# Loading w1 on ScalarE's DMA queue behind x's second half, and x's fourth half directly behind the third

## The reference

```python
q_emb = relu(q @ W3 + b3)
c = relu(((n * v + sum_over_sequence(v)) * q_emb[:, None, :]) @ W2 + b2)      # v = x, n = 32
def ternary_quant(w):
    s = mean(abs(w))
    return clip(round(w / s), -1, 1) * s
h1 = c @ ternary_quant(w1).T                                                  # w1, w3: 682 x 256
h3 = c @ ternary_quant(w3).T
x = x + (silu(h1) * h3) @ ternary_quant(w2).T                                 # w2: 256 x 682
```

## Time and profile before

| | |
|---|---|
| time, median of 3 runs | 165.83 us (165.24 to 166.05) |
| the profiled execution | 165.95 us, its span 164.2 us |
| TensorE (PE) busy | 159.7 us, 97% of the span |
| VectorE (DVE) busy | 116.4 us, 71% |
| ScalarE (ACT) busy | 89.6 us, 55% |
| GpSimd (POOL) busy | 55.1 us, 34% |
| granted TensorE clock | 1.000 of full speed |
| moved by DMA | 12.67 MB, 8.32 MB read and 4.19 MB written |

### The profile page before, as it was taken

How to read it: one execution, slowest core, us unless ns; L and a number is a source line. 1 busy time by engine, 2 the same in 40 slices (tenths; PEclk the granted TensorE clock), 3 DMA queues, 4 the chain that set the end, 5 groups by cost and what they waited for, 6 DMA issues and landing times.

```text
span 164.2 us, 2295 instructions
## 1 busy us (share of the span) xinstructions
PE 159.7 (97%) x764; PEld 131.1 (80%) x764; DVE 116.4 (71%) x187; ACT 89.6 (55%) x163; POOL 55.1 (34%) x53
## 2 busy tenths in 40 slices
PE   7999999999999999999999999999999999999992
PEld 4778787888887888788887888788887888788892
DVE  2566999978978891788548891888548870566863
ACT  4077888435844475345844466355744566255540
POOL 5014023402360276204841276204841266001500
PEclk9999999999999999999999999999999999999999
DMA  4997566665565589300250007000150006000063
GB/s 130 296 356 163 87 100 99 97 97 88 92 100 95 92 191 166 50 4 0 35 93 0 0 4 122 8 0 0 29 101 4 2 0 113 15 0 4 16 112 128
DMA packets 67412, 12.67 MB, mean 77 GB/s; under 512 B 63216, under 2 KB 67144, under 8 KB 67400
## 3 DMA queue, kind: packets, MB, share of 16 engines
q1 hardware_dynamic: 67248, 12.46, 38.7%
q10 hardware_dynamic: 152, 0.07, 0.1%
HBM read 8.32 MB, written 4.19 MB: 76 GB/s over the span
## 4 chain that ended last, share of the span: by engine, by line
PE 91%; DMA 4%; SPq 2%; issue 0%; DVE 0%
PE bank L538 49%; PE bank L581 21%; PE bank L469 15%; DMA xo<-in_x_dram 4%; PE bank L565 3%; PE bank L484 1%; PE bank L445 1%; SPq L212 1%; PE bank L496 0%; PE bank L478 0%; SPq L218 0%; SPq L217 0%; SPq L224 0%; SPq L216 0%; SPq L222 0%
## 5 line engine op out<-in xcount | busy, mean ns | idle before, releaser
L538 PE MATMUL bank<-c_hi,T 128*128 128x512 f32 (+1 forms) x176 | 69.2, 393 | 0.0
L538 PE MATMUL bank<-c_lo,T 128*128 128x512 f32 (+1 forms) x176 | 68.8, 391 | 0.0
L389 ACT ACTIVATE silu<-bank,checked 128x512 f32<-128x512 f32 (+1 forms) x48 | 33.1, 690 | 51.5 <-PE bank L538 51.3
L778 DVE SCALAR_TENSOR_TENSOR gf<-bank,out_scale,silu 128x512 f32<-128x512 f32 (+1 forms) x42 | 31.3, 744 | 34.7 <-PE bank L538 31.0
L538 PEld LDWEIGHTS bank<-c_hi,T 128*128 128x128 f32 (+1 forms) x176 | 32.8, 186 | 7.6 <-issue 0.2
L538 PEld LDWEIGHTS bank<-c_lo,T 128*128 128x128 f32 (+1 forms) x176 | 32.8, 186 | 7.3
L272 POOL TENSOR_TENSOR x<-y,qT 128x512 f32<-128x512 f32 x12 | 13.7, 1144 | 53.6 <-DVE y L685 53.6
L469 PE MATMUL bank<-x,W_sb 128*128 128x256 f32 x128 | 29.5, 381 | 0.4 <-DMA W_sb<-in_L_cond_W_dram 0.4
L581 PE MATMUL bank<-g_hi,T 128*128 128x512 f32 x70 | 28.5, 407 | 0.0
L786 DVE TENSOR_TENSOR g_lo<-gf,g_hi 128x512 fp32r<-128x512 f32 x40 | 28.5, 712 | 0.0
L581 PE MATMUL bank<-g_lo,T 128*128 128x512 f32 x70 | 27.3, 390 | 0.0
(11 more groups left out here) (78 smaller groups left out, 108.8 us busy)
## 6 DMA issues: line engine op xcount, KB each, us to landing
xb<-in_x_dram SPq DMA_DIRECT2D x64, 64.0 KB, 2.7
out_dram<-turned SPq DMA_DIRECT2D x28, 128.0 KB, 2.7
xo<-in_x_dram SPq DMA_DIRECT2D x3, 256.0 KB, 4.7
w_sb<-in_L_ffn_w_dram SPq DMA_DIRECT2D x2, 384.0 KB, 6.3
w_sb<-in_L_ffn_w_dram SPq DMA_DIRECT2D x1, 682.0 KB, 8.4
w_sb<-in_L_ffn_w_dram SPq DMA_DIRECT2D x2, 256.0 KB
xo<-in_x_dram SPq DMA_DIRECT2D x1, 512.0 KB, 4.9
xo<-in_x_dram SPq DMA_DIRECT2D x2, 128.0 KB, 2.5
```

Source lines behind the costliest of these rows:

```text
L389: nc.scalar.activation(silu[r, m % 2, :], h1[j % 2][r], ACT.Silu, scale=checked[r, 0:1]).then_inc(silu_done, 1)
L538: last = pe.matmul(dst[j % 2][0:w, :], T13[:, k, col:col + w], part[:, g % NC, k, :], start=(i == 0), stop=(i == len(passes) - 1))
L778: nc.vector.scalar_tensor_tensor(out=gf[r, m % 3, :], in0=second, scalar=out_scale[r], in1=silu[r, m % 2, :], op0=ALU.mult, op1=ALU.mult). ...
```

## The change

w1's three DMAs leave SyncE's queue. ScalarE issues them after its copy of the transposed condition, once the buffers' tails are cleared and half 1 of x has landed. On SyncE's queue half 3 of x now comes directly behind half 2, ahead of the wait for the cleared tails, and w3, w2 and the small pieces of x follow. The function that issues a matrix gets the queue as an argument.

```diff
+        def load_w13(queue, w_sb, w, got):
+            cut = LOADED * P
+            queue.dma_start(w_sb[:, 0:LOADED, :], w[0:cut, :].rearrange("(j p) d -> p j d", p=P)).then_inc(got[0], 16)
+            queue.dma_start(w_sb[:, LOADED:HC, :], w[cut:HC * P, :].rearrange("(j p) d -> p j d", p=P)).then_inc(got[1], 16)
+            queue.dma_start(w_sb[0:HR, HC, :], w[HC * P:H, :]).then_inc(got[1], 16)
...
             load_half(2)
+            load_half(3)
 
             sp.wait_ge(zeroed, 2)
-            load_w13(w1_sb, w1, got_w1)
-            load_half(3)
-            load_w13(w3_sb, w3, got_w3)
+            load_w13(sp, w3_sb, w3, got_w3)
...
             nc.scalar.copy(condT[:], condT_ps).then_inc(condT_copied, 1)
+            act.wait_ge(zeroed, 2)
+
+            act.wait_ge(got_half[0], 16)
+            load_w13(act, w1_sb, w1, got_w1)
             act.wait_ge(b_cols_copied, 1)
```

More of the change, by code:

```diff
@@ L212, in load_half @@
                 sp.dma_start(kept(g)[:, h * HTT:(h + 1) * HTT], x_v[g, :, h * HTT:(h + 1) * HTT]).then_inc(got_half[n - 1], 16)
[L214 to L218, removed]
             sp.dma_start(kept(0)[:, 0], x_v[0, :, 0]).then_inc(got_first[0], 16)
```

## The result

The changed kernel takes 172.78 us (median of 6 runs, 171.60 to 173.38) against 165.76 for the kernel before (6 runs beside it, 165.08 to 166.05). The ratio is 1.041 (95% interval 1.039 to 1.044): 7.0 us slower. The profiled execution took 173.38 us, its span 171.6; that is 7.4 more than the profiled one of before.

A forecast was written before the change was run, and what follows sets the result against it. TensorE, without a gap from 17 us, was taken to bound the kernel, so only the start-up counts. w1's later landing adds 0.65 us, other terms nothing: 165.83 + 0.65 = 166.48, predicted as 166.5 us, range 165.6 to 167.6.

The forecast's parts named there:

- w1 whole at L = 11.75: Start-up loads: w1's second part lands at 11.75 us, against 10.69 at the latest before; slack ended at 11.10.
- The bound: TensorE has no gap from 17 us on, so moving the first hidden product moves the end by the same amount.
- Half 3: Half 3 issued directly behind half 2 ends the wait before `mix_x(3)`, worth at most 0.19 us; not added to the sum.
- SyncE's issues at no cost: SyncE issues w3, w2 and the pieces of x 1.6 us earlier; transfers bind, so cost and gain are 0.
- w1 issued at 5.3 can land its first data at about 7.2: ScalarE's queue: delay before w1's first data, taken from the condition's 64 KB, which took 2.1 us.
- So I take equal shares: ScalarE's and SyncE's queues share the DMA engines equally, from 41.3% and 40.8% at 2.1 to 2.3 us; w1 whole at 11.95.
- The step from w1 to the end: With L = 11.75, w3's second sum starts at 14.25 and `sum_partitions(1)` moves from 14.68 to 15.33: +0.65 us.
- the starved rival: Rival in which w1 lands only with w3 at 13.6: +2.5 us, 168.3 us; chance 0.10.
- w1 falls behind w3: Rival: SyncE's waiting queue goes first, w1 lands only with w3 at 13.6, +2.5 us, 168.3 us; chance 0.10.
- Half 2 falls behind w1: Rival: ScalarE's fresh queue is preferred, half 2 lands at about 9.95 and delays `mix_x(2)`, +0.9 us, 166.7 us; chance 0.12.
- the same bytes must move before w3 is whole: Start-up loads: bytes to move until all of w3 is there are unchanged, so w3's end stays at 13.6 us.
- the range from 165.9 to 166.9: The forecast case's own range, for L from 11.2 to 12.2, with a third said to lie beyond 166.66.

The follow-up runs named there:

- the order alone: Changed kernel with w1 moved back to SyncE's queue, issued after half 3 of x and before w3: 165.72 us, ratio 1.000 to the kernel before.
- the kernel with TensorE kept busy: Changed kernel plus 19 matmuls on a blank tile on TensorE between `mix_x(3)` and the first sum: 169.95 us, ratio 1.026.
- the kernel that issues early: Changed kernel without ScalarE's wait for half 1 of x before it issues w1: 167.28 us, ratio 1.010.
- the run with the empty queue: Changed kernel with ScalarE issuing w1 once half 3 has landed, and SyncE issuing w3 and all behind it only once w1 is there: 169.99 us.

## Why the prediction was wrong

I had forecast 166.5 us, and it was 172.78. The term that carried the forecast was w1 whole at L = 11.75; it was whole at 15.6. It went wrong at two steps: w1's data was taken to start 2 us after its issue, whatever SyncE had issued before, and then to get half of the bytes. The sum also had no term for TensorE's clock.

**The bound: right.** TensorE has no gap behind the first hidden product, and the delay of that product, 7.40 us, is the loss of the profiled execution.

**Half 3: right.** `mix_x(3)` follows `project_c(1)` with no wait, and the order alone moves the time by nothing.

**SyncE's issues at no cost: wrong in what it left out.** Issuing w3 and w2 1.6 us earlier is no gain, as said. But it is what puts w3 ahead of w1, because in these runs the issue time decides the order between the queues as well. I had put SyncE's earlier issues at 0; holding w3, with w2 and the pieces of x behind it, back by 2.8 us (w3 from 4.26 to 7.03) gives all 7 us back, where holding back w2 and the pieces alone gives back 5.0. This is the step that failed first.

**"w1 issued at 5.3 can land its first data at about 7.2": wrong.** It rested on a DMA that had nothing ahead of it. The first packet moved at 8.6, behind w3.

**"So I take equal shares": wrong in kind.** The row between 2.1 and 2.3 us showed equal time, but it also showed 50 packets to 25; with packets of unlike size in that stretch it could not carry the assumption. Against the tail of w3, with equal packets, w1 gets its half or more (210 packets to 111 from 9 to 10 us). Against w2 it gets 30% of the bytes. I had assumed all of w3 and w1 to be through before w2 mattered; with w1 starting late, w2 and then the pieces of x are what it meets. Together: w1 whole at 15.6 where I had 11.75, with 11.95 as the worse end.

**The step from w1 to the end: right in order, wrong in size.** From w1 whole at 15.62 to the second sum's start I would have had 15.62 + 3.58 = 19.20; the trace has 21.09. The missing 1.9 us, and 1.0 more up to the first hidden product, are the lower clock; at 1.00, in the kernel with TensorE kept busy, they are gone. No term of the sum allowed that a wait of 4 us would cost 3 us more behind it. Waits of the size that was forecast left the clock at full (0.62 us in the kernel that issues early), but the price of the starved rival needed that term.

**The rivals.** "w1 falls behind w3" is what happened, at a chance of 0.10, and its price of 2.5 us had neither the share of w2 and the pieces of x nor the clock. Its one argument, the head start of SyncE's queue, should have counted most. The prediction gave that queue up to 2 MB waiting; by the trace of the changed kernel it was 1.2 MB at 5.54 us (2.21 issued, 181 GB/s x 5.54 us = 1.00 moved), and that was enough. "Half 2 falls behind w1" exists too, but for an earlier issue: issued at 3.56, w1 delays W2 and half 2, and with its own lateness that costs 1.5 us in all. That the same bytes must move before w3 is whole kept me from seeing that w3 itself would come too early, its first part at 4.26 + 5.7 = 10.0 instead of 12.5, at w1's expense.

**Two slips in the working**, neither of which moves the forecast. A half-2 landing of 9.06 is where that rival begins to cost; it passes 0.83 us only at 14.68 + 0.83 - 5.62 = 9.89. And 0.27 of the 1.0 us of the range from 165.9 to 166.9 lies beyond 166.66, where the text has a third and counts 0.35.

## What to carry to other kernels

Moving a load to a second queue did not move it forward here: what the first queue had issued by then still went first. So count the bytes issued ahead of a load on every queue, and hold back the loads that are needed later. Against loads issued later, bytes went by packet size where the two queues were compared (10 to 12 us), so expect a load with short rows to lose to one with long rows. And where a change gives TensorE waits of some us (4.2 us here, 0.86 and 1.84 in the run with the empty queue), look at the granted clock behind them: the work there may have to be priced at half clock.

## What was not expected of the hardware

- A load issued on ScalarE's queue at 5.54 us moved its first packet at 8.6 with 1.2 MB of earlier loads outstanding; with none, its first packet moved 1.0 us after its issue.
- Side by side, the queues moved 234 and 212 packets in 2 us, with 0.23 and 0.53 MB; with shorter rows on the second (SyncE's), 429 and 350 packets, with 0.43 and 0.22 MB.
- After 4.2 us without work TensorE's granted clock was 0.50 for some 6.5 us, though it was busy from 16.7 on; a `project_c` took 3.76 us instead of 1.97. In the profiled execution of the kernel in which w2 waits for w1, a wait of 1.54 us was followed by a clock of 1.00; the longest run of that kernel had a mean of 0.99. In the run with the empty queue waits of 0.86 and 1.84 us, with 2.4 us of work between them, were followed by 0.50 from 18.5 to 21 us.
